# A state-space stage regrouped: phases of eight heads by half the batches, a joined operand for high and low parts

## What is computed

```
proj = layernorm(x) @ W_in.T            # values, gates, B, C (one pair per head), dt
val  = silu(conv4(val) + conv_b)        # per feature, 4 taps, causal
cum  = cumsum(softplus(dt + dt_bias) * -exp(A_log))
M    = (C @ B.T) * exp(cum_l - cum_m)   # l >= m, per head and batch
y    = (M @ val + D * val) * silu(gate)
x    = x + y @ W_out.T
```

## Time and profile before

| | us |
| --- | --- |
| median of 3 runs | 1514.3 |
| lowest and highest | 1512.18, 1514.98 |
| the profiled execution | 1511.51 |
| its span, first to last instruction | 1509.7 |
| TensorE busy, matmuls | 1440.3 (95%) |
| VectorE, ScalarE, GpSimd busy | 897.9, 864.4, 814.3 |

### The profile page before, as it was taken

The page is one execution under the profiler, slowest core; times in us unless marked ns, Lnnn a source line. Parts: engine busy times, 40 slices in busy tenths (PEclk is TensorE's granted clock), DMA queues, the critical chain, the costliest instruction groups (busy, mean ns, idle before and its releaser), DMA issues. The chain is left out here.

```text
span 1509.7 us, 25668 instructions
## 1 busy us (share of the span) xinstructions
PE 1440.3 (95%) x8514; PEld 1248.8 (83%) x8520; DVE 897.9 (59%) x1713; ACT 864.4 (57%) x1735; POOL 814.3 (54%) x685
## 2 busy tenths in 40 slices
PE   7799899899998999999899999999999989999998
PEld 5589799798886778888689999999999986778886
DVE  5776666667665433434776676767776764433434
ACT  4566565666654433333587777777777754333332
POOL 4754344444442455555367666666667633455553
PEclk9999999999999999999999999999999999999999
DMA  2123233233221111110222112221222011111111
GB/s 81 28 71 72 59 66 77 51 75 68 69 43 39 53 43 46 48 48 25 77 75 67 58 53 58 70 63 49 56 76 63 14 36 39 42 42 52 42 51 39
DMA packets 48600, 82.38 MB, mean 55 GB/s; under 512 B 4256, under 2 KB 29984, under 8 KB 48288
## 3 DMA queue, kind: packets, MB, share of 16 engines
q1 hardware_dynamic: 48544, 81.70, 20.0%
HBM read 80.38 MB, written 1.31 MB: 54 GB/s over the span
## 5 line engine op out<-in xcount | busy, mean ns | idle before, releaser
L392 POOL TENSOR_TENSOR ms_a_lo<-m_a,ms_a_hi 128x384 fp32r<-128x384 f32 x128 | 130.2, 1017 | 211.6 <-ACT ms_a_hi L388 211.5
L1085 DVE TENSOR_TENSOR f_h<-f_sc,ps 128x512 f32<-128x512 f32 x112 | 76.2, 681 | 184.8 <-POOL f_sc L1017 184.8
L243 PE MATMUL ps<-xn_hi,fgu_hi 128*128 128x512 f32 x448 | 178.1, 398 | 5.3 <-DVE f_h L1085 5.3
L245 PE MATMUL ps<-xn_hi,fgu_lo 128*128 128x512 f32 x448 | 178.6, 399 | 0.0
L244 PE MATMUL ps<-xn_lo,fgu_hi 128*128 128x512 f32 x448 | 177.5, 396 | 0.0
L1087 DVE TENSOR_TENSOR fh_lo<-f_h,fh_hi 128x512 fp32r<-128x512 f32 x112 | 107.9, 963 | 99.2 <-ACT fh_hi L388 99.2
L966 ACT ACTIVATE f_s<-ps 128x512 f32<-128x512 f32 x112 | 66.7, 598 | 162.5 <-PE ps L245 162.4
L1017 POOL TENSOR_TENSOR f_sc<-f_s,coef_r 128x512 f32<-128x512 f32 x88 | 113.9, 1295 | 67.7 <-ACT f_s L966 67.7
L388 ACT CAST fh_hi<-f_h 128x512 fp32r<-128x512 f32 x112 | 69.0, 616 | 125.0 <-DVE f_h L1085 124.9
L392 POOL TENSOR_TENSOR fd_lo<-fw_raw,fd_hi 128x256 fp32r<-128x256 f32 x56 | 51.2, 914 | 125.6 <-ACT fd_hi L388 125.6
L243 PE MATMUL ps<-xn_hi,aw_hi 128*128 128x512 f32 x256 | 109.9, 429 | 7.4 <-DVE bmat_lo L698 7.2
(11 more groups left out here) (276 smaller groups left out, 4894.9 us busy)
## 6 DMA issues: line engine op xcount, KB each, us to landing
fw_raw<-ffn_w SPq DMA_DIRECT2D x56, 384.0 KB, 3.0
rows_a<-a_rows_d SPq DMA_DIRECT2D x64, 256.0 KB, 4.8
wconv_raw<-b_conv SPq DMA_DIRECT2D x16, 513.0 KB, 3.6
aw_raw<-a_heads SPq DMA_DIRECT2D x32, 256.0 KB, 5.1
wvo_raw<-b_vo SPq DMA_DIRECT2D x16, 512.0 KB, 3.4
rows_b<-b_rows_d SPq DMA_DIRECT2D x32, 256.0 KB, 4.8
wqk_raw<-b_qk SPq DMA_DIRECT2D x16, 256.0 KB, 4.8
x<-xT SPq DMA_DIRECT2D x2, 512.0 KB, 5.5
```

The costliest lines, as they stand in the source:

```text
L243: nc.tensor.matmul(o, w[0], v[0], start=first, stop=False, skip_group_check=True)
L245: return nc.tensor.matmul(o, w[1], v[0], start=False, stop=last, skip_group_check=True)
L392: return nc.gpsimd.tensor_tensor(dst[1], src, f32(dst[0]), ALU.subtract).then_inc(sem(done_sem), 1)
L1085: nc.vector.tensor_tensor(f_h[:, c], f_sc[:, c], ps[:, 2 + c, :], ALU.mult).then_inc(sem("f_h"), 1)
```

## The change

A step is now one head for half the batches (two units), and a phase is eight heads for one half: eight phases of 16 units. Two projections per step, B in the even unit and C in the odd one, always for the next step, 512 tokens each; bmat, cmat, yT and ys are half as wide. The exponents and decays of a unit are made one unit earlier.

valz holds both parts in one stationary operand: four heads' high parts in one half of its 128 columns, their low parts in the other, so a half-phase of four heads fills it. A value product is three matmuls of 256 columns (high and low part of M for the first block of rows, then both parts of the second block side by side). The output has the low part's share in the other 64 partitions. ScalarE copies those to y_lo, and VectorE's `a_sum_dve` adds D * val, the two shares and the second block's column range in three instructions, four times a phase. The copy of the transposed values to val_tok is ScalarE's, valz's low part GpSimd's; stage is gone.

All groups are written out, no loop is left in this stage. There are 16 output products. The fourth convolution tile is on VectorE. All eight heads of a group keep their weights in aw. In the layer norm `prepare_first` comes behind the cast of the first half.

```diff
+SUM_UNITS, YS_UNIT, OUT_UNITS = (1, 2), 3, (7, 10)
+VALZ_UNITS, T_UNIT, AWO_UNIT = (2, 11), 4, 13
...
-            prepare_first(act)
             for c in range(CHUNKS):
                 for k in range(KT):
                     act.wait_ge(sem("ln_xn"), KT * (CHUNKS * n + c) + k + 1)
                     nc.scalar.copy(xn[0][:, k, cols(c)], ln_xc[:, k, cols(c)]).then_inc(sem("ln_hi"), 1)
+                if c == 0:
+                    prepare_first(act)
...
+        def fill_of(k):
+            g, c, j = of_step(k)
+            if g == 0 and c == 0:
+                return j + 2 if j + 2 < A_GROUP else None
+            late = k - 2 * A_GROUP * (g - 1 + c) - A_GROUP
+            return (g + c) * A_GROUP + FILL_AT.index(late) if late in FILL_AT and g + c < A_TILES else None
+
+        FILL_AT = (0, 2, 4, 6, 8, 10, 11, 12)
...
-            if b % 2 == 0:
-
-                pe.wait_ge(sem("bc_split"), UNITS * g + 4 * j + 3 + b // 2)
-            s = ps[:, 4 + u % 2, :]
+                pe.wait_ge(sem("a_m_done"), u - 1)
+            if b == 0:
+                pe.wait_ge(sem("bc_split"), 2 * k + 2)
+            s = ps[:, 4 + b, :]
...
+            o, ms = ps[:, 6 + b, :], at(ms_a, slice(None), u % 3)
+            for i, m in enumerate(ms):
+                nc.tensor.matmul(half_view(o[:, 0:SEQ]), valz[:, n % 2, j, 2 * b], first_m(m), start=j == 0 and i == 0,
+                                 stop=False, skip_group_check=True)
+
+            nc.tensor.matmul(half_view(o[:, P:TRI]), valz[:, n % 2, j, 2 * b + 1], ms_a[2][:, :, u % 3, P:2 * P], start=False,
+                             stop=j == A_HALF - 1, skip_group_check=True).then_inc(sem("a_y_done"), 1)
+
+        def a_phase_pe(pe, p):
+
+            for n in range(PHASE_UNITS):
+                u = PHASE_UNITS * p + n
                 if u > 0:
-                    a_state_pe(pe, g, u)
...
+                    a_state_pe(pe, u)
+                if u // 2 + 1 < STEPS:
+                    a_project_pe(pe, u // 2 + 1, u % 2)
+                if n == T_UNIT and p + 1 < PHASES:
+                    a_transpose_pe(pe, p + 1)
+                if n in OUT_UNITS and p > 0:
+                    a_out_pe(pe, p - 1, OUT_UNITS.index(n), 3)
                 if u >= 2:
-                    a_value_pe(pe, g, u - 2)
...
+        def a_sum_dve(dve, step, n, b):
+
+            rows, t, c = half_rows(n % 2), n // 4, n // 2 % 2
+            l0 = c * CHUNK + b * SEQ
+            y, o = yT[rows, b * SEQ:(b + 1) * SEQ], ps[rows, 6 + b, :]
+            dve.wait_ge(sem("a_y_done"), HALF_UNITS * (n + 1) - 2 + b + 1)
+            step(nc.vector.scalar_tensor_tensor(y, valT[rows, t, l0:l0 + SEQ], a_d[rows, t:t + 1], o[:, 0:SEQ], ALU.mult, ALU.add))
+            nc.vector.tensor_tensor(y[:, P:SEQ], y[:, P:SEQ], o[:, SEQ:TRI], ALU.add).then_inc(sem("y_read"), 1)
+            dve.wait_ge(sem("y_read"), 2 * n + b + 1)
+            dve.wait_ge(sem("lo_read"), 2 * n + b + 1)
+            nc.vector.tensor_tensor(y, y, y_lo[rows, b * SEQ:(b + 1) * SEQ], ALU.add).then_inc(sem("lo_added"), 1)
```

More of the change, by code:

```diff
@@ L117, in build_layer @@
         ma = ExitStack()
[L118 to L122, removed]
+        valz = sb(ma, "valz", [P, 2, A_HALF, CHUNK_BLOCKS, P], FR)
+        val_tok = sb(ma, "val_tok", [P, CHUNK_BLOCKS, P])
+        y_lo = sb(ma, "y_lo", [P, CHUNK])
+        ys = pair(ma, "ys", [P, CHUNK])
         pro = ExitStack()
@@ new lines, in a_valz_act, with a_lo_act @@
+        def a_valz_act(act, n):
+            if n == 0:
+                act.wait_ge(sem("valz_zero"), 1)
+            if n >= 2:
+                act.wait_ge(sem("a_y_done"), HALF_UNITS * (n - 1))
+            act.wait_ge(sem("val_tok"), n // 2 + 1)
+            nc.scalar.copy(valz_diagonal(n % 2, 0), val_of(n % 2)).then_inc(sem("valz_hi"), 1)
+        def a_lo_act(act, n, b):
+            act.wait_ge(sem("a_y_done"), HALF_UNITS * (n + 1) - 2 + b + 1)
+            if n >= 2:
+                act.wait_ge(sem("lo_added"), 2 * (n - 2) + b + 1)
+            nc.scalar.copy(y_lo[half_rows(n % 2), b * SEQ:(b + 1) * SEQ],
+                           ps[half_rows(1 - n % 2), 6 + b, 0:SEQ]).then_inc(sem("lo_read"), 1)
@@ new lines, in a_phase_pool @@
+        def a_phase_pool(pool, p):
+            for n in range(PHASE_UNITS):
+                u = PHASE_UNITS * p + n
+                split_lo(pool, at(ms_a, slice(None), u % 3), m_a[:, u % 2, :], "a_m_hi", u + 1, "a_m_split")
+                if n == VALZ_UNITS[0]:
+                    a_valz_pool(pool, 2 * p + 1)
+                if n == VALZ_UNITS[1] and p + 1 < PHASES:
+                    a_valz_pool(pool, 2 * p + 2)
+                if u % 2 == 1 and fill_of(u // 2) is not None:
+                    a_fill_pool(pool, fill_of(u // 2))
+                if n == AWO_UNIT and p % 2 == 0:
+                    split_lo(pool, at(awo, slice(None)), awo_raw[:], "awo_hi", p // 2 + 1, "awo_split")
@@ new lines, in a_sp @@
+            sp.wait_ge(sem("rows_stored"), 16)
+            for k in range(3):
+                a_rows_sp(sp, k)
+            for h in range(2, 4):
+                a_fill_sp(sp, h)
+            for k in range(STEPS):
+                g, c, j = of_step(k)
+                if c == 0 and j == 0:
+                    if g > 0:
+                        sp.wait_ge(sem("awo_split"), g)
+                    sp.dma_start(awo_raw[:], a_wo[g * P:(g + 1) * P, :]).then_inc(sem("awo_loaded"), 16)
+                if k + 3 < STEPS:
+                    sp.wait_ge(sem("a_e_done"), 2 * k + 2)
+                    a_rows_sp(sp, k + 3)
+                if fill_of(k) is not None and fill_of(k) + 2 < A_HEADS:
+                    a_fill_sp(sp, fill_of(k) + 2)
```

512 lines of the change are left out of this document (231 added, 281 removed).

## The result

The changed kernel takes 1640.3 us (median of four runs, 1635.2 to 1640.6) against 1513.4 for the kernel before (four runs): ratio 1.083, 95% interval 1.0806 to 1.0854. The forecast was 1603 us, with a range of 1530 to 1650: the sign and the mechanism hold, the size was 37 us short.

A forecast was written before the change was run, and what follows sets the result against it. TensorE was taken to bound the middle of the stage before, and the wait for C's low part after. Stage +80.8, prologue -13, norms -3, stage end -1.3 and clock +25.5 on 1514.3 gave 1603 us, range 1530 to 1650.

The forecast's parts named there:

- (b): State-space stage: next state product waits for C's low part, so a step takes 6.25 us instead of 5.56.
- (a): Value product: three matmuls instead of six, 0.35 us instead of 0.63, 36 us of TensorE's work gone.
- (c): VectorE's sums, gate and x additions ahead of C's low part: +7.06 us a phase in seven phases, 2.25 in the first.
- (i): TensorE's clock: falls after long pauses, 30 places, half taken, 15 x 1.7 us, +25.5 us.
- (d): First group's weights: TensorE waits 1.3 us for aw's low part in six steps, 7.8 us.
- (e): Written-out groups: the 4.3 us gap and lower clock at the loop's return fall away, twice; not counted separately.
- (f): Prologue: convolution of tile 3 goes to VectorE, first m_a comes at about 58.8 us, -13 us.
- (g): Layer norm: weight casts move behind the first half's cast, -1 us in each of three norms, -3; a further one in (f).
- (h): End of the stage: last sum half as wide, two last output products instead of four, -1.3 us.
- Rival 1: C's low part is there in time and TensorE stays packed: 1455 us, faster; chance 0.10.
- Rival 3: The chain of (b) alone, with (c) and (d) finding room and the clock up: 1518 us, up to 1545; chance 0.18.
- Rival 2: The clock falls at nearly every step's pause, short ones too: 109 us instead of 25.5, 1687 us; chance 0.12.

The follow-up runs named there:

- e1_shift: Changed kernel with every projection of the state-space stage one place earlier: 1535.3 us, ratio 1.0123 to the kernel before.
- e10_cast2: Changed kernel with one more ScalarE copy of C's bank, 64 times, ahead of the cast that makes cmat_hi: 1678.7 us, ratio 1.1088.
- e3_fill: Changed kernel with zero matmuls put where TensorE waits for C's low part: 1603.8 us, ratio 1.0582 to the kernel before.
- e6_pad: Changed kernel with earlier projections, y_lo copied first and weight splits of heads 2 and 3 made early, plus two zero matmuls per unit: 1485.7 us.
- e4_unroll: Kernel before with only the loop over its groups written out on all five engines: 1499.7 us, ratio 0.9896.
- e7_ln: Kernel before with only the layer norm's part, first weight casts behind the casts of the first half: 1510.4 us, ratio 0.9973.
- e8_best_noln: Changed kernel with earlier projections, y_lo copied first, early weight splits, and the layer norm's part undone: 1462.8 us, against 1461.9 with that part.
- e9_gate: Changed kernel with earlier projections, y_lo copied first, early weight splits, and the gate moved from unit 2 to unit 3: 1449.4 us, ratio 0.9572.
- e2_ylo: Changed kernel with ScalarE's y_lo copy moved ahead of its cast of the projection in units 1, 2, 9 and 10: 1563.8 us, ratio 1.0322.

## Why the prediction was right, and where it was short

- **What bounds, and (b), the chain.** Right. The plain step was put at 6.25 us and is 6.26; the wait has the name, the line and the count that were forecast, 1.14 us at the shortest for 1.3. e1_shift takes it away in the plain step, e10_cast2 lengthens it, e3_fill shows that work of TensorE's put into it costs nothing.
- **(a), the value product.** The size is right: a product takes 0.36 us (from 257.59 in the rows above to the state product at 257.95). Half of them stand in the pause and gain nothing (e3_fill); the other half shorten the chain, which the sum of (b) has in it and no run tests. With cover it is worth 24 us for all (e6_pad).
- **(c), the queue ahead of C's low part: mis-sized.** 7.06 us a phase were forecast. With the clock out of the way (e3_fill), the steps exceed its plain 6.20 us by 2.27 (units 0-1), 2.78 (2-3), 1.17 (6-7), 2.15 (8-9) and 2.10 (10-11), 10.5 us. Unit 7 is right at 1.2. Each of the other four has a sum, and there the step "So it runs at 6.17 to 6.59" failed: the add was taken at 0.42 us, the gate at 0.69, as they run alone; beside GpSimd they take 0.87 and 1.11. These are 4 x 0.45 + 0.42 = 2.2 of the 3.4 us. For the rest I have only a guess, the longer queue ahead of them and at unit 10 the output product, which I let the pause cover in part. Stage without the clock: 456.2 forecast, 480.3 measured (516.2 less the clock's 35.9; e3_fill itself has 476.5).
- **(i), the clock: the price right, the number short.** A fall costs 1.6 us, where 1.7 were forecast; there are 23, not 15. 36 us against 25.5. "of which I take half" was the step that failed: of the 27 pauses above 2.3 us (for 24 forecast) 21 were followed by a fall, and two falls came behind shorter ones. It is tied to (c), whose pauses were longer than forecast (2.9 to 3.9 us at units 1, 2 and 9 after the first phase, not 2.7 to 2.9).
- **(d)** 7.8 us were put down for the first phase's weights; the waits for aw_lo are 4.5 us in four, not six. The first phase takes 63.4 us in e3_fill, where the forecast's terms give 59. What it had not is the wait of 4.6 us in the very first step (the longest in the first row of the waits): TensorE has both projections done by then, but ScalarE comes to their casts only behind the first decays and the values' copies.
- **(e)** Right: e4_unroll, 11.2 us in the stage for 12.
- **(f)** Right: first m_a at 59.1, forecast 58.8. But one first pass took 3.80 us instead of 0.75, where GpSimd clears valz, and the rest made it up: that the sum came out to 0.3 us is luck, although the three later tiles take 13.9 us for the 14.1 forecast.
- **(g), (h)** -4.3 us were forecast for all behind the stage's last m_a, and the two profiles show +0.6. e7_ln gives the 3.9 us of (g) as a difference of medians, while its one profile has 1064.3 us behind the last m_a. A single profile can't tell a term of this size. In the regrouped kernel the runs of e8_best_noln don't show (g) either: there the part is worth 0.9 us or nothing, not 4. (h) was not tried alone.
- **The rivals.** Rival 1 asked for 1.3 us of other work between C's projection and its reader, and put the time at 1455. The changed kernel doesn't have it; e9_gate has, and takes 1449: the condition was the right one, the change as made didn't meet it. Rival 3 put the chain without (c) and the clock at 1518; no run has exactly that. Rival 2, a fall in every pause, did not come: in e2_ylo the plain steps keep their pauses of 1.1 us, and over 60 us with nine such or somewhat longer pauses the granted clock is 1.00. But that only long pauses take the clock down is wrong as well: in the same kernel a pause of 1.7 us was followed by a fall in six of seven phases. First the 60 us, then one of the six:

```profile
360.00:420.00 60.00, 47.87 (x282) 41.17 (x281) 38.62 (x87) 35.28 (x86) 25.92 (x25) 1.00 0.29 61
```
```profile
183.00 0.35 PE L244 MATMUL ps<-cmat_hi,bmat_hi 128*128 128x256 f32 x1 [1.71 <-DVE cmat_lo L741]
...
184.63 0.63 PE L244 MATMUL ps<-xn_hi,aw_hi 128*128 128x512 f32 x1
```

The errors add up: +24.1 us from (c) and (d), +10.4 from (i), +5.2 from (f) to (h), together 39.7 of span, against 37 between forecast and median. All three go one way, so the 1640 lie above what the forecast gave as its own case (1560 to 1630); the range to 1650 holds them because it reached into rival 2.

## What to carry to other kernels

When a change moves a producer closer to its reader, time the whole path from the last matmul to the operand (1.75 us here) and count what stands between them in TensorE's list; work saved beside that path is worth nothing while the path is longer. Then walk each in-order engine on the path: an operation that waits for another engine and sits ahead of the critical one costs its wait in full once the slack ahead of the critical one is used up, and four lines moved in ScalarE's list were worth 76 us. An element-wise operation must be priced by whom it runs beside, and a pause of two or three microseconds on TensorE by the clock that it can take down as well.

## What the runs showed of the hardware

- VectorE's operations with both tensors in SBUF stretch when GpSimd works at the same time: the 64x256 add from 0.42 to 0.87 us, the 128x512 gate from 0.69 to 1.11 and up to 1.51. With one tensor in PSUM there is no change: in the changed kernel m_a takes 0.54 to 0.56 us with GpSimd at work and without, and in e9_gate the 64x128 add, L767 above, takes 0.28 to 0.29 in 12 cases beside GpSimd and in 20 alone. The Trainium skill (SBUF — State Buffer, "SBUF: two separate sides") says that a pair of SBUF ports is shared by VectorE and GpSimd and held for a whole instruction, also by a VectorE operation with two SBUF inputs against one of GpSimd that reads SBUF. The rows agree with it: from 60 to 460 in the changed kernel all 23 late adds that have a row of their own start 0.4 us after a split of GpSimd's has begun, and end 0.3 us after its end. They don't show which engine held the ports.
- A pause of 1.1 us in every step left the granted clock at its upper level. Behind the first phase, pauses of 1.4 us (e2_ylo) never did either and pauses of 1.6 us did once in seven (changed kernel), but 1.7 us did in six of seven phases (e2_ylo) and 2.0 and 2.8 us in all seven (e1_shift), to 1.2 GHz; in the changed kernel pauses of 3.3 and 3.4 us left it up four times of 14. So the length of a pause doesn't settle it alone. The matmuls may slow down only a microsecond and a half after the work has begun again (263.97 to 265.43 above), and a fall costs about 1.6 us.
- Zero matmuls in a pause hold the clock at 1.00, and the run with them was 36 us faster, in a kernel that was waiting anyway. Once the waits are gone there is nothing for them to do: e9_gate is at 1.00 without any.
- Where a loop over all five engines goes back, TensorE stood still for 4.3 us and the clock fell; with the groups written out the stage is 5.6 us shorter for each time.
